# The third layer of four single experts as three passes of split fp32 in a fused attention and expert kernel

## The chip, the cores and the metric

The kernel runs on one core of a Trainium2 chip. The metric is the device time of one execution in microseconds: before the change, 740.17 us as the median of three runs (739.69 to 741.97).

## The reference

The input x is 2 x 2048 tokens of 512 values. Four blocks add to it in turn; the change touches the last.

```python
x = x + _L0_xattn_ref(_layernorm(x), ctx, ctx, mask, ...)   # cross attention with relu
x = x + _L0_ffn_ref(_layernorm(x), weight, bias)             # fp6-quantised product
x = x + _L1_xattn_ref(_layernorm(x), ctx, W, b)              # one 512x512 product and a mean
x = x + _L1_ffn_ref(_layernorm(x), Wg, bg, w1, b1, w2, b2, w3, b3)

def _L1_ffn_ref(x, Wg, bg, w1, b1, w2, b2, w3, b3):          # 16 experts
    probs = softmax(x @ Wg + bg, axis=tokens)
    vals, idx = top_k(probs per batch and expert, 128)
    tok = x[idx]                                             # 128 tokens per batch and expert
    h = relu(tok @ w1[e] + b1[e])
    h = relu(h @ w2[e] + b2[e])
    h = h @ w3[e] + b3[e]
    outputs.at[idx].add(h * vals)
```

Every expert is three 512x512 products on 128 tokens of each of the two batches, all in fp32 accuracy.

## The kernel before, in words

The first 410 us compute the three attention-like blocks tile by tile and the gate's logits; what follows are the experts. There are two kinds of work in the expert phase.

**Joint experts.** Twelve experts (numbers 4 to 15, called e = 0 to 11 in the code, `JOINT` of them) run with the tokens of both batches side by side, 256 columns. Each fp32 operand is split into a high and a low part of a reduced fp32 type (`F32R`): ScalarE writes the high part (`split_hi` for weights, line 1505; the second `activation` of `relu`, line 1907, for hidden values), VectorE subtracts it from the original for the low part (`split_lo`, `hidden_lo`, line 1982). A product is then `three_passes` (line 350): high by high, high by low, low by high, three matmuls for each of the four chunks of 128. The weights pass through a ring: the list `order` (line 504) names each weight matrix, `load_raw` brings item i of it into one of `RAW` = 3 raw buffers as soon as item i-3 has been split, and its halves go into `WR` = 5 pairs of buffers.

**Single experts.** Experts 0 to 3 have run already for one batch with unsplit fp32 matmuls. For the other batch they are put, one each, into the turns e = 1, 4, 7 and 9 (`SINGLE`, line 550): 128 tokens, three layers, all unsplit fp32 (`single_first`, `single_second`, `single_outputs`, lines 1409 to 1433). Their weights come into the buffers `w_e` by `load_single` (line 706) and are used as they land. `single_relu` (line 1914) on ScalarE makes the input of the next layer.

**Order of the work.** Nothing is scheduled by a planner; each engine runs its list in the order in which it is written, and semaphores tie the lists. TensorE in turn e: `single_tokens`, `hidden(e, 0)`, `single_first`, `tokens(e + 1)`, `outputs(e - 1)`, `single_second`, `hidden(e, 1)`, `single_outputs` (the four single parts only where e is in `SINGLE`). ScalarE in turn e: one weight split, the two relus of layer 0, `single_relu(.., 0)`, the tokens of e+1, a weight split, `single_relu(.., 1)`, a weight split, the relus of layer 1, `single_weighted`. VectorE in turn e: a weight split, `hidden_lo` twice, `token_lo(e + 1)`, then twice a weight split followed by `weighted(e - 1, b)`, then `hidden_lo` twice. `single_outputs` writes the bank that `weighted(e - 1, 1)` reads, so it waits for that (`d_y`, line 1428); the semaphore `a_sv` tells TensorE that ScalarE has made the single expert's values. GpSimd gathers tokens and adds results into the output with indirect DMAs; the program ends with the adds of e = 11.

Of the kernel before, what the change touches and what calls it, by code (L numbers as in the profile page):

```python
# [27 lines left out]
F32R = mybir.dt.float32r  # L28
# [4 lines left out]
ACT = mybir.ActivationFunctionType  # L33
AX_X = mybir.AxisListType.X

P = 128
# [9 lines left out]
FIRST = 4  # L46


def build(nc, io):
    B, S, D = io.x.shape  # L50
# [3 lines left out]
    C = D // P  # L54
# [28 lines left out]
        g_zero c_bcol k_full k_max k_top k_cand k_got k_half k_moved k_ids k_sum k_exp k_tr k_out k_pos a_soft  # L83
        a_w d_w g_w p_tok a_thi d_tlo a_h d_hlo p_h p_y d_y
        c_cut a_chain e_dve e_pe e_act e_pool e_logit
        p_ev a_ev p_sv a_sv s_gather
    """.split()
    sm = namedtuple("Semaphores", sem_names)(*[ctx.enter_context(nc.semaphore(n)) for n in sem_names])
    XR = 10
    RAW = 3  # L90
# [7 lines left out]
    sem_raw = [ctx.enter_context(nc.semaphore(f"raw_in{i}")) for i in range(RAW)]  # L98
# [9 lines left out]
    top = [-(-nc.sbuf_base // 64) * 64]  # L108

    def place(name, shape, dt=F32, at=None):  # L110

        size = int(np.prod(shape[1:])) * mybir.dt.size(dt)
        off = top[0] if at is None else at
        if at is None:
            top[0] = off + -(-size // 32) * 32
        return nc.alloc_sbuf_tensor_at(name, shape, dt, offset=off)
# [15 lines left out]
    b1 = place("b1", [P, E])  # L132
    b2 = place("b2", [P, E])
# [73 lines left out]
    KB = 1024  # L207
# [67 lines left out]
    w_h, w_l, w_raw = [], [], []  # L275
# [16 lines left out]
    h2_s = place("single_h2", [P, D], at=at_lists + 2 * KB)  # L292
# [2 lines left out]
    exps = place("exps", [P, GT])  # L295
    top[0] = at_qt
    tok_h, tok_l = place("tokT_h", [P, C, B * P], F32R), place("tokT_l", [P, C, B * P], F32R)
    tokT_s, h1_s = place("single_tokT", [P, D]), place("single_h1", [P, D])
    h32 = [place(f"h32_{i}", [P, 2 * B * P]) for i in range(2)]
    assert top[0] == at_x2  # L300
    for i in range(2, WR):
# [34 lines left out]
    def chunked(w):  # L336

        return w.rearrange("(c p) n -> p c n", p=P)
# [11 lines left out]
    def three_passes(pe, out, pairs):  # L350

        last = None
        n = 0
        for a_h, a_l, b_h, b_l in pairs:
            for a, b in ((a_h, b_h), (a_h, b_l), (a_l, b_h)):
                last = pe.matmul(out, a, b, start=(n == 0), stop=(n == 3 * len(pairs) - 1))  # L356
                n += 1
        return last
# [142 lines left out]
    GS = counts("half mean k01 k23 wf_0 wf_1 wf_2 wf")  # L501


    order = [(0, 0), (0, 1)]
    for e in range(1, JOINT):
        order += [(e, 0), (e - 1, 2), (e, 1)]
    order += [(JOINT - 1, 2)]
    when = {w: i for i, w in enumerate(order)}
    AHEAD = 3
# [37 lines left out]
    RING = (0, 1, 4, 2, 3)  # L547
    slots_in = ((sem_cut[0], 16 * (GB // 2) + 16), (sem_cut[1], 16 * (GB // 2) + 16), (sem_copies, 32), (sem_slots, 16))
    EV = counts("t0 t1 a0 a1 b0 b1 t2 y0 t3 y1 a2 a3 b2 b3 y2 y3")
    SINGLE = {1: 0, 4: 1, 7: 2, 9: 3}  # L550

    def first_adds(e):

# [21 lines left out]
    def used(eng, i):  # L575

        e, layer = order[i]
        if layer == 2:
            eng.wait_ge(sm.p_y, B * (e + 1))
        else:  # L580
            eng.wait_ge(sm.p_h, 4 * e + 2 * layer + 2)
# [5 lines left out]
    def _(sp):  # L587
# [110 lines left out]
        def load_raw(i):  # L698
            e, layer = order[i]
            if i >= RAW:  # L700
                sp.wait_ge(sm.a_w, i - RAW + 1)
                lo_done(sp, i - RAW)
            sp.dma_start(w_raw[i % RAW][:, :, :], chunked(io.w[layer][FIRST + e])).then_inc(sem_raw[i % RAW], 16)

        def load_single(s, layer):

            i = 3 * s + layer
            if i < 4:
                sp.wait_ge(sm.p_ev, EV["y3"])
            else:  # L710
                at, was = divmod(i - 4, 3)
                sp.wait_ge(sm.p_sv, 4 * at + was + 2)
            sp.dma_start(w_e[i % 4][:, :, :], chunked(io.w[layer][s])).then_inc(sem_early[i % 4], 16)

# [25 lines left out]
        for i in range(RAW + 1, len(order)):  # L740
            load_raw(i)
            for u, s in SINGLE.items():
                if i == max(when[(u, 0)], RAW + 1):
                    load_single(s, 0)
                    load_single(s, 1)
                if i == when[(u, 1)]:
                    load_single(s, 2)
        for b in range(B):
            sp.wait_ge(sem_add[b], 16 * E)

# [2 lines left out]
    def _(pe):  # L753
# [644 lines left out]

        def late_weights(s, layer):

            i = 3 * s + layer
            pe.wait_ge(sem_early[i % 4], 16 * ((3, 3, 2, 2)[i % 4] + i // 4 + 1))
            return w_e[i % 4]

# [19 lines left out]

        def single_outputs(s, u):

            w = late_weights(s, 2)
            pe.wait_ge(sm.d_y, B * u)
            pe.wait_ge(sm.a_sv, 4 * s + 3)
            for d in range(C):  # L1430
                last = pe.matmul(ps_y[1][:, :], h2_s[:, d * P:(d + 1) * P], w[:, d, :],  # L1431
                                 start=(d == 0), stop=(d == C - 1))
            last.then_inc(sm.p_sv, 1)

        def last_outputs():

# [30 lines left out]
        wh, _ = weights(0)  # L1467
# [27 lines left out]
    def _(act):  # L1495
# [392 lines left out]
        def token_hi(e):  # L1888
            for b in range(B):
                act.wait_ge(sm.p_tok, B * e + b + 1)  # L1890
                act.wait_ge(sm.p_h, max(0, 4 * (e - 1) + 2))
                for part in token_parts(e, b):
                    hi(sm.a_thi, tok_h[:, part, b * P:(b + 1) * P], in4(token_bank(e, b, part.start))[:, part, :])
# [20 lines left out]
        def single_relu(s, layer):  # L1914

            act.wait_ge(sm.p_sv, 4 * s + 2 + layer)
            act.activation((h1_s, h2_s)[layer][:, :], ps_hid[2 + layer][:, :], ACT.Relu,
                           bias=(b1, b2)[layer][:, s:s + 1]).then_inc(sm.a_sv, 1)

        def single_weighted(s, u):  # L1920

# [9 lines left out]
        for e in range(JOINT):  # L1931
            if nxt < len(order) and e > 0:
                split_hi(nxt)
                nxt += 1
            if e in SINGLE:
                single_copy(SINGLE[e])
            if e == 0:
                act.wait_ge(sem_add[0], 16 * 2)
            relu(e, 0, 0)
            relu(e, 0, 1)  # L1940
            if e in SINGLE:
                single_relu(SINGLE[e], 0)
            if e + 1 < JOINT:
                token_hi(e + 1)
            for n in range(2):
                if nxt < len(order) and (e > 0 or n == 1):
                    split_hi(nxt)
                    nxt += 1
                if n == 0 and e in SINGLE:
                    single_relu(SINGLE[e], 1)  # L1950
            if e == 0:
                act.wait_ge(sem_add[0], 16 * FIRST)
            relu(e, 1, 0)
            relu(e, 1, 1)
            if e in SINGLE:
                single_weighted(SINGLE[e], e)
# [4 lines left out]
    def _(dve):  # L1961
# [19 lines left out]
        def lo(sem, dst, src, hi_part):  # L1981
            dve.tensor_tensor(dst, src, hi_part, ALU.subtract).then_inc(sem, 1)  # L1982
# [554 lines left out]
        def split_lo(i):  # L2537
            dve.wait_ge(sm.a_w, i + 1)
            lo(sm.d_w, w_l[i % WR][:, :, :], w_raw[i % RAW][:, :, :], w_h[i % WR][:, :, :])

        def token_lo(e):
            for b in range(B):
                t = slice(b * P, (b + 1) * P)
                for i, part in enumerate(token_parts(e, b)):
                    dve.wait_ge(sm.a_thi, B * e + b + 1 + (i if e == 0 else 1))
                    lo(sm.d_tlo, tok_l[:, part, t], in4(token_bank(e, b, part.start))[:, part, :], tok_h[:, part, t])

        def hidden_lo(e, layer, pair):
            n = 4 * e + 2 * layer + pair
            dve.wait_ge(sm.a_h, n + 1)  # L2550
            src = h32[n % 2][:, :].rearrange("p (a t) -> p a t", a=2)
            part = slice(2 * pair, 2 * pair + 2)
            lo(sm.d_hlo, h_l[layer][:, part, :], src, h_h[layer][:, part, :])

        def weighted(e, b):

            dve.wait_ge(sm.p_y, B * e + b + 1)
            if e >= 2:
                dve.wait_ge(sem_add[b], 16 * (first_adds, second_adds)[b](e - 2))
            expert = FIRST + e  # L2560
            r = b * E + expert
            dve.tensor_scalar(y[e % 2][b][:, :], ps_y[b][:, :], b3[:, expert:expert + 1], vals[:, r:r + 1],  # L2562
                              ALU.add, ALU.mult).then_inc(sm.d_y, 1)
# [3 lines left out]
        nxt = 2  # L2567
        for e in range(JOINT):
            if nxt < len(order) and e > 0:
                split_lo(nxt)  # L2570
                nxt += 1
            hidden_lo(e, 0, 0)
            hidden_lo(e, 0, 1)
            if e + 1 < JOINT:
                token_lo(e + 1)
            for n in range(2):
                if nxt < len(order):
                    split_lo(nxt)
                    nxt += 1
                if e >= 1:  # L2580
                    weighted(e - 1, n)
            hidden_lo(e, 1, 0)
            hidden_lo(e, 1, 1)
        e = JOINT - 1
# [360 lines left out]
```

## Time and profile before

| what | value |
|---|---|
| median of three runs | 740.17 us (739.69 to 741.97) |
| the profiled execution | 738.98 us, of which the span is 737.2 us |
| TensorE busy | 714.1 us (97%) |
| VectorE busy | 520.4 us (71%) |
| ScalarE busy | 402.0 us (55%) |
| GpSimd busy | 421.6 us (57%) |
| granted TensorE clock, mean | 0.993 |

The span runs from the first instruction to the last of the profiled execution; 1.78 us of the execution lie around it. A row of a timeline has the start, the length, the engine (PE is TensorE, PEld its weight loads, DVE VectorE, ACT ScalarE, POOL GpSimd, SPq the queue of SyncE), the line of the kernel and the tiles (out<-in); in brackets stands idle time of the engine ahead of it and what ended it. Instructions on one engine overlap by a little, so the distance between two starts is shorter than the length. `banks` is the pair of accumulator banks 6 and 7, `early_w` the buffers `w_e`, and `single_h` the tiles `h1_s` and `h2_s`.

### The profile page before, as it was taken

The numbers are of one execution on the slowest core, as the hardware profiler recorded it, in microseconds if no ns is written. First come the engines' busy times: TensorE is split into PE (matmuls) and PEld (weight loads), VectorE is DVE, ScalarE is ACT, GpSimd is POOL, SyncE is SP. The second block draws the span as 40 slices with busy tenths as digits, with TensorE's granted clock in tenths as the row PEclk, the third lists the DMA queues.
The fourth block names the chain that finished last, engine by engine and source line by source line (L and its number), as shares of the span: only waits on it lengthen the run. The fifth ranks groups of instructions, "written<-read, shape, count | busy, mean of one in ns | idle before, by whom it ended". The sixth has DMA issues, their size and how long they took to land.

```text
span 737.2 us, 12752 instructions
## 1 busy us (share of the span) xinstructions
PE 714.1 (97%) x4506; PEld 623.2 (85%) x4506; DVE 520.4 (71%) x978; ACT 402.0 (55%) x680; POOL 421.6 (57%) x621
## 2 busy tenths in 40 slices
PE   6999999999999999999999899999999999999995
PEld 5765888888888888888888878798999899899894
DVE  5785789889888898875897798463664556363561
ACT  5755444454554445868668533454664556464641
POOL 2825789888888887876878722604430442340132
PEclk9999999999999999999999999999999999999998
DMA  8710122222212213110116998796895798995544
GB/s 311 267 30 15 44 73 76 76 85 73 89 60 87 86 58 103 44 61 29 61 60 242 334 401 296 191 366 186 234 372 165 192 355 268 298 274 157 143 86 58
DMA packets 61671, 118.04 MB, mean 160 GB/s; under 512 B 6056, under 2 KB 7464, under 8 KB 61608
## 3 DMA queue, kind: packets, MB, share of 16 engines
q1 hardware_dynamic: 54312, 100.44, 38.9%
q0 software_dynamic: 7296, 16.78, 10.3%
q8 instruction: 37, 0.61, 0.3%
q14 instruction: 26, 0.21, 0.1%
HBM read 91.76 MB, written 25.21 MB: 159 GB/s over the span
## 4 chain that ended last, share of the span: by engine, by line
PE 84%; issue 5%; DMA 3%; DVE 3%; POOL 2%; ACT 2%; POOLq 0%; DVEq 0%; ACTq 0%
PE bank L356 39%; PE banks L356 9%; PE bank L363 6%; PE bank L1004 6%; PE banks L871 4%; PE banks L877 3%; DMA out<-y,ids 3%; PE banks L1004 2%; PE banks L881 2%; PE banks L882 2%; PE banks L1431 1%; PE bank L1326 1%; PE banks L1035 1%; PE bank L1048 1%; DMA tok<-xn,ids 0%
## 5 line engine op out<-in xcount | busy, mean ns | idle before, releaser
L2851 POOL DMA_INDIRECT out<-y,ids x24 | 46.1, 1923 | 156.8 <-DVE y L2562 155.0
L1982 DVE TENSOR_TENSOR w_l<-w_raw,w_h 128x2048 fp32r<-128x2048 f32 x35 | 80.1, 2290 | 62.8 <-ACT w_h L1505 58.5
L1970 DVE BATCH_NORM_STATS2 bn<-x 128x6 f32<-128x512 f32 x112 | 77.0, 687 | 8.0 <-DMA x<-x 5.2
L1505 ACT ACTIVATE w_h<-w_raw 128x2048 fp32r<-128x2048 f32 x36 | 68.5, 1918 | 7.1 <-DMA w_raw<-w 7.1
L1901 ACT ACTIVATE h<-bank,b 128x512 f32<-128x512 f32 x48 | 33.1, 689 | 63.0 <-PE bank L356 60.0
L1982 DVE TENSOR_TENSOR hT_l<-h,hT_h 128x512 fp32r<-128x512 f32 x48 | 33.0, 690 | 40.3 <-ACT hT_h L1907 38.1
L356 PE MATMUL bank<-tokT_h,w_h 128*128 128x256 f32 x188 | 55.1, 293 | 0.0
L356 PE MATMUL bank<-tokT_h,w_l 128*128 128x256 f32 x188 | 53.2, 283 | 0.0
L356 PE MATMUL bank<-tokT_l,w_h 128*128 128x256 f32 x188 | 53.2, 283 | 0.0
L2614 POOL TENSOR_SCALAR rstd<-mean_var 128x1 f32<-128x1 f32 x108 | 25.9, 239 | 47.2 <-DVE mean_var L1975 42.2
L356 PE MATMUL bank<-wf_h,xdT_h 128*128 128x512 f32 x128 | 52.7, 412 | 0.0
L356 PE MATMUL bank<-wf_h,xdT_l 128*128 128x512 f32 x128 | 50.3, 393 | 0.0
L356 PE MATMUL bank<-hT_h,w_h 128*128 128x256 f32 x176 | 50.1, 285 | 0.0
L356 PE MATMUL bank<-wf_l,xdT_h 128*128 128x512 f32 x128 | 50.0, 390 | 0.0
L356 PE MATMUL bank<-hT_l,w_h 128*128 128x256 f32 x176 | 49.8, 283 | 0.0
L356 PE MATMUL bank<-hT_h,w_l 128*128 128x256 f32 x176 | 49.8, 283 | 0.0
L1659 ACT ACTIVATE q<-bank,bq 128x512 f32<-128x512 f32 x32 | 22.1, 689 | 45.0 <-PE bank L356 44.5
L2694 POOL TENSOR_TENSOR x<-x,mix_bias 128x512 f32<-128x512 f32 x32 | 41.4, 1293 | 1.9 <-PE bank L363 1.7
L2632 POOL TENSOR_TENSOR qT_l<-q,qT_h 128x512 fp32r<-128x512 f32 x32 | 41.5, 1297 | 0.8 <-ACT qT_h L1661 0.8
L2730 POOL TENSOR_TENSOR x<-x,ffn_bias 128x512 f32<-128x512 f32 x32 | 41.9, 1309 | 0.0
L1501 ACT ACTIVATE xn<-x,rstd 128x512 f32<-128x512 f32 x32 | 26.1, 816 | 24.6 <-POOL rstd L2629 19.6
L1982 DVE TENSOR_TENSOR xdT_l<-bank,xdT_h 128x512 fp32r<-128x512 f32 x32 | 22.0, 689 | 23.9 <-ACT xdT_h L1505 23.7
(426 smaller groups left out, 2377.3 us busy)
## 6 DMA issues: line engine op xcount, KB each, us to landing
w_raw<-w SPq DMA_DIRECT2D x36, 1024.0 KB
early_w<-w SPq DMA_DIRECT2D x24, 1024.0 KB, 10.6
x<-x SPq DMA_DIRECT2D x32, 256.0 KB, 2.8
xn<-xn SPq DMA_DIRECT2D x32, 256.0 KB
out<-x SPq DMA_DIRECT2D x29, 256.0 KB, 2.5
mask<-mask_t SPq DMA_DIRECT2D x8, 256.0 KB, 3.3
slot_all<-slots SPq DMA_DIRECT2D x4, 512.0 KB, 7.8
stage<-wk SPq DMA_DIRECT2D x1, 1024.0 KB, 7.8
```

What stands on the lines that cost most here:

```text
L356: last = pe.matmul(out, a, b, start=(n == 0), stop=(n == 3 * len(pairs) - 1))
L363: last = pe.transpose(bank[:, c * P:(c + 1) * P], src[:, c * P:(c + 1) * P], ident[:, :])
L871: last = pe.matmul(both_halves[:, a, 0:WIDE], xh[:, d, :], wc_h[:, d, a, :], start=(d == 0), stop=(d == C - 1))
L1004: last = pe.matmul(bank[:, c * P:(c + 1) * P], w[:, d, c * P:(c + 1) * P], x[:, d * P:(d + 1) * P], start=(d == 0), stop=(d == C - 1))
L1505: act.activation(dst, src, ACT.Copy).then_inc(sem, 1)
L1901: act.activation(h32[n % 2][:, :], ps_hid[n % 4][:, :], ACT.Relu, bias=bias)
L1970: dve.bn_stats(bn6[which][:, j % 2, :], src[:, :]).then_inc(sem_bn[which], 1)
L1982: dve.tensor_tensor(dst, src, hi_part, ALU.subtract).then_inc(sem, 1)
L2632: pool.tensor_tensor(dst, src, hi_part, ALU.subtract).then_inc(sem, 1)
L2694: pool.tensor_tensor(x2[j % 2][:, :], x2[j % 2][:, :], cbias[:, batch(j), :], ALU.add).then_inc(sm.g_x2b, 1)
L2730: pool.tensor_tensor(x1_of(k)[:, :], x1_of(k)[:, :], fbias[:, :], ALU.add).then_inc(sm.g_x1b, 1)
L2851: pool.indirect_dma_start(out=out_rows, out_offset=bass.IndirectOffsetOnAxis(ap=ids[:, r:r + 1], axis=0), in_=y[e % 2][b][:, :], in_offset ...
```

## The change

The third layer of the four single experts is computed by `three_passes` instead of four unsplit fp32 matmuls. Its weight matrix becomes an item of the ring's list, `(e, ALONE)`, just behind `(e, 1)`; the separate load of it goes, and `w_e` then holds two matrices for each single expert (`3 * s + layer` becomes `2 * s + layer` in `load_single` and `late_weights`, and the divisor there 2). ScalarE and VectorE each split one more matrix in each of the four turns. `single_relu(.., 1)` writes its result twice, as fp32 and as the high half, and the new `single_lo` on VectorE makes the low half. The two new tiles lie over `tokT_s` and `h1_s`, which are free by then. TensorE waits for `single_lo` by the new semaphore `d_sv`.

```diff
     tokT_s, h1_s = place("single_tokT", [P, D]), place("single_h1", [P, D])
+    h2_s_h = place("single_h2_h", [P, D], F32R, at=at_single)
+    h2_s_l = place("single_h2_l", [P, D], F32R, at=at_single + 2 * KB)
...
+    SINGLE = {1: 0, 4: 1, 7: 2, 9: 3}
+    ALONE = 3
     order = [(0, 0), (0, 1)]
     for e in range(1, JOINT):
         order += [(e, 0), (e - 1, 2), (e, 1)]
+        if e in SINGLE:
+            order.append((e, ALONE))
     order += [(JOINT - 1, 2)]
...
         e, layer = order[i]
-        if layer == 2:
+        if layer == ALONE:
+            eng.wait_ge(sm.p_sv, 4 * SINGLE[e] + 4)
+        elif layer == 2:
             eng.wait_ge(sm.p_y, B * (e + 1))
...
-            sp.dma_start(w_raw[i % RAW][:, :, :], chunked(io.w[layer][FIRST + e])).then_inc(sem_raw[i % RAW], 16)
+            w = io.w[2][SINGLE[e]] if layer == ALONE else io.w[layer][FIRST + e]
+            sp.dma_start(w_raw[i % RAW][:, :, :], chunked(w)).then_inc(sem_raw[i % RAW], 16)
...
                     load_single(s, 0)
                     load_single(s, 1)
-                if i == when[(u, 1)]:
-                    load_single(s, 2)
...
         def single_outputs(s, u):
 
-            w = late_weights(s, 2)
+            wh, wl = weights(when[(u, ALONE)])
             pe.wait_ge(sm.d_y, B * u)
-            pe.wait_ge(sm.a_sv, 4 * s + 3)
-            for d in range(C):
-                last = pe.matmul(ps_y[1][:, :], h2_s[:, d * P:(d + 1) * P], w[:, d, :],
-                                 start=(d == 0), stop=(d == C - 1))
-            last.then_inc(sm.p_sv, 1)
+            pe.wait_ge(sm.d_sv, s + 1)
+            f = [slice(d * P, (d + 1) * P) for d in range(C)]
+            three_passes(pe, ps_y[1][:, :], [(h2_s_h[:, f[d]], h2_s_l[:, f[d]], wh[:, d, :], wl[:, d, :])
+                                             for d in range(C)]).then_inc(sm.p_sv, 1)
...
             act.wait_ge(sm.p_sv, 4 * s + 2 + layer)
-            act.activation((h1_s, h2_s)[layer][:, :], ps_hid[2 + layer][:, :], ACT.Relu,
-                           bias=(b1, b2)[layer][:, s:s + 1]).then_inc(sm.a_sv, 1)
+            last = act.activation((h1_s, h2_s)[layer][:, :], ps_hid[2 + layer][:, :], ACT.Relu,
+                                  bias=(b1, b2)[layer][:, s:s + 1])
+            if layer == 1:
+                last = act.activation(h2_s_h[:, :], ps_hid[3][:, :], ACT.Relu, bias=b2[:, s:s + 1])
+            last.then_inc(sm.a_sv, 1)
...
             if e + 1 < JOINT:
                 token_hi(e + 1)
+            if e in SINGLE:
+                split_hi(nxt)
+                nxt += 1
             for n in range(2):
...
+        def single_lo(s):
+
+            dve.wait_ge(sm.a_sv, 4 * s + 3)
+            lo(sm.d_sv, h2_s_l[:, :], h2_s[:, :], h2_s_h[:, :])
+
...
             if e + 1 < JOINT:
                 token_lo(e + 1)
+            if e in SINGLE:
+                split_lo(nxt)
+                nxt += 1
             for n in range(2):
                 if nxt < len(order):
                     split_lo(nxt)
                     nxt += 1
                 if e >= 1:
                     weighted(e - 1, n)
+            if e in SINGLE:
+                single_lo(SINGLE[e])
             hidden_lo(e, 1, 0)
             hidden_lo(e, 1, 1)
```

On ScalarE, in turn e = 1 between the tokens of e = 2 and the relus of layer 1, before. `single_h_248` is the second layer's result of the single expert, `w_h` the high halves of weights, `w_raw` the ring's raw buffers.

```order
L1505 ACTIVATE tokT_h<-bank 128x4x128 [waits p_h,p_tok] x2
L1505 ACTIVATE w_h_226<-w_raw_229 128x2048 [waits p_h,raw_in2]
L1917 ACTIVATE single_h_248<-bank,b_64 128x512 [waits p_sv]
L1505 ACTIVATE w_h_228<-w_raw_225 128x2048 [waits p_h,raw_in0]
L1901 ACTIVATE h_0_257<-bank,b_64 128x512 [waits d_hlo,p_h]
L1907 ACTIVATE hT_h_222<-bank,b_64 128x512 [waits p_y]
```

The same place after the change:

```order
L1511 ACTIVATE tokT_h<-bank 128x4x128 [waits p_h,p_tok] x2
L1511 ACTIVATE w_h_226<-w_raw_229 128x2048 [waits p_h,raw_in2]
L1511 ACTIVATE w_h_228<-w_raw_225 128x2048 [waits p_h,raw_in0]
L1923 ACTIVATE single_h_248<-bank,b_64 128x512 [waits p_sv]
L1926 ACTIVATE single_h_h<-bank,b_64 128x512
L1511 ACTIVATE w_h_230<-w_raw_227 128x2048 [waits p_h,raw_in1]
L1907 ACTIVATE h_0_259<-bank,b_64 128x512 [waits d_hlo,p_h]
L1913 ACTIVATE hT_h_222<-bank,b_64 128x512 [waits p_y]
```

An instruction for `single_h_h` now stands between the single expert's relu and the split of the last weight matrix of the turn; the matrix that the single expert's third layer needs is split ahead of both (the first `w_h` of the second list).

On VectorE, in the same turn, before. `w_l` are the low halves of weights, `y` the scaled results of e = 0 for the two batches, `hT_l` the low halves of layer 1's values.

```order
L1982 TENSOR_TENSOR tokT_l<-bank,tokT_h 128x4x128 [waits a_thi] x2
L1982 TENSOR_TENSOR w_l_231<-w_raw_229,w_h_226 128x2048 [waits a_w]
L2562 TENSOR_SCALAR y_235<-banks,b_65,vals 128x512 [waits p_y]
L1982 TENSOR_TENSOR w_l_232<-w_raw_225,w_h_228 128x2048 [waits a_w]
L2562 TENSOR_SCALAR y_236<-banks,b_65,vals 128x512 [waits p_y]
L1982 TENSOR_TENSOR hT_l_224<-h_0_257,hT_h_222 128x512 [waits a_h]
L1982 TENSOR_TENSOR hT_l_224<-h_1_258,hT_h_222 128x512 [waits a_h]
```

After the change:

```order
L1994 TENSOR_TENSOR tokT_l<-bank,tokT_h 128x4x128 [waits a_thi] x2
L1994 TENSOR_TENSOR w_l_231<-w_raw_229,w_h_226 128x2048 [waits a_w]
L1994 TENSOR_TENSOR w_l_232<-w_raw_225,w_h_228 128x2048 [waits a_w]
L2579 TENSOR_SCALAR y_235<-banks,b_65,vals 128x512 [waits p_y]
L1994 TENSOR_TENSOR w_l_261<-w_raw_227,w_h_230 128x2048 [waits a_w]
L2579 TENSOR_SCALAR y_236<-banks,b_65,vals 128x512 [waits p_y]
L1994 TENSOR_TENSOR single_h_l<-single_h_248,single_h_h 128x512 [waits a_sv]
L1994 TENSOR_TENSOR hT_l_224<-h_0_259,hT_h_222 128x512 [waits a_h]
L1994 TENSOR_TENSOR hT_l_224<-h_1_260,hT_h_222 128x512 [waits a_h]
```

One more weight split stands ahead of the first `y`, and `single_h_l` stands behind the second `y`, that is, behind the split of the turn's last weight matrix. The same holds in the turns e = 4, 7 and 9.

## Rows read from the trace of the kernel before

**Rows 1.** The page: span, engine totals, granted clock in 40 slices (tenths).
```profile
span 737.2 us, 12752 instructions
PE 714.1 (97%) x4506; PEld 623.2 (85%) x4506; DVE 520.4 (71%) x978; ACT 402.0 (55%) x680; POOL 421.6 (57%) x621
...
PEclk9999999999999999999999999999999999999998
```

**Rows 2.** The chain that ended last: start us, length us, what; single expert 0's turn.
```profile
501.56 5.75 PE bank L356 x48
507.32 3.60 PE banks L1431 x8
...
517.54 5.46 PE banks L356 x24
```

**Rows 3.** Timeline, TensorE, entry into the single product: start, length, engine, line, operation.
```profile
507.04 0.28 PE L356 MATMUL bank<-hT_h,w_l 128*128 128x256 f32 x1
507.21 0.30 PEld L1431 LDWEIGHTS banks<-early_w,single_h 128*128 128x128 f32 x2
507.24 3.67 PE L1431 MATMUL banks<-early_w,single_h 128*128 128x512 f32 x8
```

**Rows 4.** Timeline, TensorE: first and twelfth of the 24 products of outputs(8).
```profile
668.63 0.47 PE L356 MATMUL banks<-w_h,hT_h 128*128 128x512 f32 x1
...
671.24 0.39 PE L356 MATMUL banks<-w_h,hT_l 128*128 128x512 f32 x1
```

**Rows 5.** Timeline, ScalarE, the same turn.
```profile
501.60 0.69 ACT L1917 ACTIVATE single_h<-bank,b 128x512 f32<-128x512 f32 x1 [6.45 <-PE bank L1004]
502.19 1.90 ACT L1505 ACTIVATE w_h<-w_raw 128x2048 fp32r<-128x2048 f32 x1
504.48 0.69 ACT L1901 ACTIVATE h<-bank,b 128x512 f32<-128x512 f32 x1 [0.39 <-PE bank L356]
```

**Rows 6.** Timeline, VectorE, the same turn.
```profile
504.12 2.29 DVE L1982 TENSOR_TENSOR w_l<-w_raw,w_h 128x2048 fp32r<-128x2048 f32 x1 [5.92 <-ACT w_h L1505]
506.33 0.81 DVE L2562 TENSOR_SCALAR y<-banks,b,vals 128x512 f32<-128x512 f32 x1
507.05 0.68 DVE L1982 TENSOR_TENSOR hT_l<-h,hT_h 128x512 fp32r<-128x512 f32 x1
```

**Rows 7.** Timeline, VectorE and TensorE, turn e = 4.
```profile
571.08 0.81 DVE L2562 TENSOR_SCALAR y<-banks,b,vals 128x512 f32<-128x512 f32 x1
...
571.96 0.30 PEld L1431 LDWEIGHTS banks<-early_w,single_h 128*128 128x128 f32 x2
```

**Rows 8.** Timeline and windows: a restart of TensorE behind VectorE.
```profile
468.66 0.41 DVE L1982 TENSOR_TENSOR tokT_l<-bank,tokT_h 128x256 fp32r<-128x256 f32 x1
...
469.18 0.19 PEld L1353 LDWEIGHTS bank<-tokT_h,w_h 128*128 128x128 f32 x1 [0.81 <-issue]
...
468.00:470.00 2.00, 1.60 (x11) 1.15 (x10) 1.95 (x4) 0.66 (x2) 1.70 (x3) 1.00 0.79 209
```

**Rows 9.** Timeline (SyncE, ScalarE) and windows: weight loads and where the queue runs empty.
```profile
523.56 1.05 SPq L713 DMA_DIRECT2D early_w<-w  x2
...
526.07 0.37 SPq L703 DMA_DIRECT2D w_raw<-w  x1
...
541.50 1.91 ACT L1505 ACTIVATE w_h<-w_raw 128x2048 fp32r<-128x2048 f32 x1 [2.91 <-DMA w_raw<-w]
...
552.15 0.37 SPq L703 DMA_DIRECT2D w_raw<-w  x1
...
557.00:562.00 5.00, 5.00 (x25) 4.15 (x24) 3.35 (x3) 2.90 (x4) 0.00 (x0) 1.00 0.13 49
```

**Rows 10.** Timeline, VectorE and GpSimd: the end of the program.
```profile
728.01 0.54 DVE L2590 TENSOR_SCALAR y<-bank,b,vals 128x256 f32<-128x256 f32 x1 [0.82 <-PE bank L1454]
728.83 1.54 POOL L2851 DMA_INDIRECT out<-y,ids  x1 [0.34 <-DVE y L2590]
```

More of the change, by code:

```diff
@@ L85, in build @@
         c_cut a_chain e_dve e_pe e_act e_pool e_logit
-        p_ev a_ev p_sv a_sv s_gather
+        p_ev a_ev p_sv a_sv d_sv s_gather
     """.split()
@@ L297, in build @@
     tok_h, tok_l = place("tokT_h", [P, C, B * P], F32R), place("tokT_l", [P, C, B * P], F32R)
+    at_single = top[0]
     tokT_s, h1_s = place("single_tokT", [P, D]), place("single_h1", [P, D])
+    h2_s_h = place("single_h2_h", [P, D], F32R, at=at_single)
+    h2_s_l = place("single_h2_l", [P, D], F32R, at=at_single + 2 * KB)
     h32 = [place(f"h32_{i}", [P, 2 * B * P]) for i in range(2)]
@@ L549, in build @@
     EV = counts("t0 t1 a0 a1 b0 b1 t2 y0 t3 y1 a2 a3 b2 b3 y2 y3")
-    SINGLE = {1: 0, 4: 1, 7: 2, 9: 3}
     def first_adds(e):
@@ L702, in load_raw @@
                 lo_done(sp, i - RAW)
-            sp.dma_start(w_raw[i % RAW][:, :, :], chunked(io.w[layer][FIRST + e])).then_inc(sem_raw[i % RAW], 16)
+            w = io.w[2][SINGLE[e]] if layer == ALONE else io.w[layer][FIRST + e]
+            sp.dma_start(w_raw[i % RAW][:, :, :], chunked(w)).then_inc(sem_raw[i % RAW], 16)
         def load_single(s, layer):
-            i = 3 * s + layer
+            i = 2 * s + layer
             if i < 4:
@@ L710, in load_single @@
             else:
-                at, was = divmod(i - 4, 3)
+                at, was = divmod(i - 4, 2)
                 sp.wait_ge(sm.p_sv, 4 * at + was + 2)
@@ L1399, in late_weights @@
         def late_weights(s, layer):
-            i = 3 * s + layer
+            i = 2 * s + layer
             pe.wait_ge(sem_early[i % 4], 16 * ((3, 3, 2, 2)[i % 4] + i // 4 + 1))
```

## The prediction

> **What bounds the kernel now.** I read the page first: TensorE is busy for 714.1 of 737.2 us, at the full clock in nearly every slice, with VectorE at 71% and ScalarE at 55% [rows 1]. Then the chain that ended last: around a single expert it goes from one group of TensorE's matmuls to the next with no other engine in it [rows 2]. So a microsecond less of matmuls there is a microsecond less at the end, as long as TensorE finds its operands ready; and a wait put ahead of TensorE costs all of itself. The question is which operand comes last in front of the single expert's third layer, so the third view is the timeline at that point.
>
> There the profile shows something that the totals hide. The last matmul of hidden(1, 1) starts at 507.04 us [rows 3], and they follow each other at 5.75 / 48 = 0.12 us [rows 2], so the next could start at 507.16. The first weight load of the third layer starts at 507.21 and its matmul at 507.24 [rows 3], after VectorE's second y, which ends at 506.33 + 0.81 = 507.14 [rows 6]. The same 0.07 us lies between y and the load in turn 4, 571.08 + 0.81 = 571.89 and 571.96 [rows 7]; the turns 7 and 9 repeat the pattern, four in all. TensorE thus already waits for y here, by some 0.08 us, once per single expert. The slack in this place is nothing; all four turns repeat it.
>
> **What TensorE saves.** The unsplit group takes 3.67 us from its first start to its last end [rows 3]. The new group is twelve matmuls of the form that outputs(e) has 24 of: 128x128 stationary, 512 columns, high and low halves. Its twelfth starts 671.24 - 668.63 = 2.61 us after the first and lasts 0.39 us, so twelve take 3.00 us from start to end [rows 4]. Saved: 0.67 us per single expert. By the chain's way of counting it is 3.60 - 5.46 / 2 = 0.87 us [rows 2], which leaves out the slower first matmul; since TensorE will restart from a wait, I take 0.67 and keep 0.87 as an end of the range.
>
> The Trainium skill ("FP8 and Floating Point Precision", TensorE Precision Notes) says that true fp32 makes four passes through the array; "TensorE: Matmul & The Clock Gate" (Back-to-back issue gap) gives N / 2.4 + 2.5 ns for one of them. By these the group goes from 16 passes to 12 of 0.216 us, 3.45 to 2.59 us, an estimated saving of 0.86 us. The trace agrees for the unsplit form (3.67 us), and shows the split form slower than the rule, 2.61 / 11 = 0.237 us per matmul. With the rule's figure the sum below would come out 0.8 us lower.
>
> **What the change puts in front of it.** TensorE now waits for d_sv, which VectorE gives after single_h_l. The order lists show single_h_l behind the second y, and that y is behind the low split of the turn's last weight matrix, which waits for ScalarE's high split, which is behind the single expert's relu. Step by step in turn 1:
> - ScalarE: the relu starts at 501.60, as before, since TensorE releases it. The next instruction started 0.59 us later [rows 5]. The added copy single_h_h takes that place, and the weight split moves from 502.19 to 502.78. It takes 1.90 and ends at 504.68.
> - VectorE: before, the low split started 504.12 - (502.19 + 1.90) = 0.03 us behind the high one; now at 504.71. y follows 506.33 - 504.12 = 2.21 us later, at 506.92, and the next instruction 507.05 - 506.33 = 0.72 us behind it [rows 6]. That is now single_h_l, at 507.64. It is the operation and shape of hT_l, 0.68 us [rows 6], and ends at 508.32.
> - TensorE: its weight load comes 0.07 us later, 508.39, and the first matmul 0.03 us after that, 508.42, instead of 507.24.
>
> So the start moves by 1.18 us: 0.59 for the copy on ScalarE and 0.59 for the subtraction behind y. The group then ends at 508.42 + 3.00 = 511.42 instead of 507.24 + 3.67 = 510.91. Each single expert costs 0.51 us more than before, though its matmuls are shorter. Nothing on TensorE behind it takes this back: it was busy from there to the next single expert, and the copy's delay of ScalarE is over when relu of layer 1 starts at 504.48 [rows 5] (the weight split, which ends at 504.68, makes it 0.2 us late at most, and nothing needs that relu before the next turn's outputs).
>
> **What is hidden.** The added weight split costs about 1.9 us on ScalarE and 2.2 on VectorE in each of the four turns. Both engines stood idle just there: 6.45 us ahead of the single relu [rows 5] and 5.92 us ahead of the low split [rows 6]. The extra split delays the first y by about 2.2 us, which goes into a GpSimd add and not to TensorE. These cost nothing. If the cover on VectorE were gone, the whole split would stand in the wait; it has 5.92 - 2.21 = 3.7 us to spare.
>
> **What the ring does.** One more item goes through it in each of these turns, and raw item i is asked for when item i-3 is split, so the loads behind the added one are asked for one place later. The tight one is the turn's last matrix, (e, 2): its load goes out when (e, 1) has been split. In turn 4, which is 571.08 - 506.33 = 64.75 us behind turn 1, a load is issued at that moment, 552.15, and ScalarE would want it at 502.78 + 64.75 = 567.53, 15.4 us later. The slowest landing I find is a load issued at 526.07 that ScalarE could use at 541.50, also 15.4 us [rows 9]. But that one had two matrices in the queue just ahead of it, issued from 523.56 on, and behind 552.15 the DMA engines are down to a share of 0.13 from 557 on [rows 9], so the load has landed about 5 us after its issue. With the separate load of the third layer gone, the queue holds no more than before. I cost it at 0, with 0 to 1 us per turn as bounds.
>
> **The sum.** 4 x (1.18 - 0.67) = +2.0 us. The end of the program hangs on TensorE: the last y ends at 728.55 and GpSimd's last add starts at 728.83, 0.34 us idle before it and released by that y [rows 10]; no single expert lies behind turn 9, so the tail moves as a whole. The profiled execution would go from 738.98 us (737.2 and 1.78 around it) to 741.0, and the median from 740.17 to 742.2. Bounds: with the chain's 0.87 the sum is 4 x 0.31 = 1.2 us. A restart of TensorE behind VectorE shows 469.18 - (468.66 + 0.41) = 0.11 us instead of 0.07 [rows 8]; with that, and 0.1 us more for the first matmul, and up to 0.1 for an instruction on ScalarE or VectorE that does not overlap, it is 4 x 0.75 = 3.0. The likeliest case alone is 741.4 to 743.2.
>
> **Rivals.**
> 1. No new wait: single_h_l is ready early and only y counts. Then the group starts at 507.16 to 507.24 and each single expert gains 0.67 to 0.87 us: 3.0 on the middle, 737.2 us. It needs the last weight split to be out of the way; the order lists speak against it. It could come true only if the releases worked otherwise than the rows say. Chance 0.07.
> 2. The ring runs dry: the load of (e, 2) lands more than 15.4 us after its issue, ScalarE's split of it waits, and behind it stand on the one line VectorE's low split, y, single_h_l and TensorE. From that point every microsecond of landing costs one, in each of four turns: at 16.4 us 4 more, 746.2 us. For it speaks the one landing of 15.4 us; against it the empty queue from 557 on. Chance 0.07.
> 3. The clock falls during the new waits. TensorE stood idle 0.81 us ahead of 469.18, and the window from 468 to 470 has a granted clock of 1.00 [rows 8], so a wait of 1.2 us should not do it. If it did, the 5.75 us of the next hidden layer [rows 2] would take twice as long once per turn: 23 us more, 765 us. Chance 0.01. The Trainium skill ("TensorE: Matmul & The Clock Gate", HAM oscillation) warns of TensorE idling for data between groups of matmuls, after which the gate throttles it again; the window from 468 to 470 does not show it.
>
> **How the numbers follow.** A measurement of this kernel can tell about 0.3%, 2.2 us, from no change. My case (chance 0.85) is +2.0 us, just inside that bound, and its own range goes over it: I give 0.50 of it to no change and 0.35 to slower. Faster is rival 1, 0.07. Slower is 0.35 + 0.07 + 0.01 = 0.43. The range goes from 740.4, below my bound of 741.4 for what the median of a few runs strays, to 744.2 on the side of rival 2.
>
> **What will show it.** In the trace after: TensorE idle by 1.1 to 1.2 us ahead of the first product of single_h_h in turns 1, 4, 7 and 9, released by single_h_l; single_h_l starting 0.7 us behind the second y; four groups of twelve matmuls of some 3.0 us; ScalarE's split of (e, 2) starting 1.2 us behind the single relu's start with no DMA wait. If TensorE runs through without idling there, rival 1 holds and the saving is real; if the waiting of w_h for w_raw has grown, rival 2; if the clock row has lower digits, rival 3. I would be wrong in the sum, not in the mechanism, if the wait is far from 1.18 us or the group from 3.0 us.

## The result, and the profile after

The changed kernel takes 742.54 us (median of 9 runs, 740.62 to 743.61), the kernel before 739.69 us beside it (9 runs). The ratio is 1.0026, 95% interval 1.0015 to 1.0038, that is +1.9 us (1.1 to 2.8). The two medians lie further apart, 2.85 us, at the upper end of that interval; in what follows the ratio is used. The interval lies above 1, so the change makes the kernel slower, but the ratio is inside the 0.3% that the prediction set as its bound for no change. The profiled execution took 741.43 us.

The page of the kernel after, its span and engine totals, answers to [rows 1]:

```profile
span 739.6 us, 12812 instructions
PE 710.6 (96%) x4522; PEld 625.1 (85%) x4522; DVE 533.2 (72%) x986; ACT 410.7 (56%) x688; POOL 420.2 (57%) x621
```

TensorE is busy for 3.5 us less than before (714.1 to 710.6), and yet the span is 2.4 us longer. Not all of the 3.5 us is the three passes' doing: two profiles of one kernel, split_first and split_first_again below, differ by 2.1 us in this number (711.7 and 709.6), and the turns below show 0.67 us less in each of four, 2.7 us. VectorE and ScalarE have 12.8 and 8.7 us more to do, most of it in time that they had.

The chain that ended last (start, length, what) in the turn of single expert 0, where the chain before had only TensorE [rows 2]:

```profile
502.61 0.68 ACT single_h_h L1926
503.29 1.81 ACT w_h L1511
505.13 2.29 DVE w_l L1994
507.42 0.72 DVE y L2579
508.14 0.61 DVE single_h_l L1994
508.75 0.14 issue
508.89 3.00 PE banks L359 x12
```

It leaves TensorE at the single expert's second relu and comes back to it through the copy, the weight split of ScalarE, VectorE's split, y and the subtraction, each behind the other: the line that the prediction laid out.

The timeline of ScalarE in that turn, for [rows 5]; the last row is the end of the single expert's turn:

```profile
502.02 0.69 ACT L1923 ACTIVATE single_h<-bank,b 128x512 f32<-128x512 f32 x1 [4.65 <-PE bank L1011]
502.61 0.68 ACT L1926 ACTIVATE single_h_h<-bank,b 128x512 fp32r<-128x512 f32 x1
503.18 1.92 ACT L1511 ACTIVATE w_h<-w_raw 128x2048 fp32r<-128x2048 f32 x1
...
511.93 0.78 ACT L1935 ACTIVATE single_y<-banks,single_bias,vals 128x512 f32<-128x512 f32 x1 [2.88 <-PE banks L359]
```

VectorE, for [rows 6]:

```profile
505.13 2.29 DVE L1994 TENSOR_TENSOR w_l<-w_raw,w_h 128x2048 fp32r<-128x2048 f32 x1 [4.30 <-ACT w_h L1511]
507.34 0.80 DVE L2579 TENSOR_SCALAR y<-banks,b,vals 128x512 f32<-128x512 f32 x1
508.06 0.68 DVE L1994 TENSOR_TENSOR single_h_l<-single_h,single_h_h 128x512 fp32r<-128x512 f32 x1
```

TensorE, for [rows 3] and [rows 4]: the last matmul of hidden(1, 1), the first weight load and matmul of the third layer, its second, and its twelfth matmul.

```profile
507.46 0.28 PE L359 MATMUL bank<-hT_h,w_l 128*128 128x256 f32 x1
...
508.86 0.19 PEld L359 LDWEIGHTS banks<-w_h,single_h_h 128*128 128x128 f32 x1 [1.32 <-issue]
508.89 0.47 PE L359 MATMUL banks<-w_h,single_h_h 128*128 128x512 f32 x1 [1.15 <-DVE single_h_l L1994]
509.19 0.39 PE L359 MATMUL banks<-w_l,single_h_h 128*128 128x512 f32 x1
...
511.50 0.39 PE L359 MATMUL banks<-w_h,single_h_l 128*128 128x512 f32 x1
```

The times are best counted from the start of the single expert's second relu, which TensorE alone releases: 501.60 before, 502.02 after. (The 0.42 us between them arise before this relu. In the ten profiles of the table below the relu starts anywhere from 501.60 to 505.60, at 504.07 in before_split_first, which has no part of the change; so I do not count them as its cost.) The first matmul of the third layer starts 6.87 us behind it, before 5.64 us: 1.23 us later. The group takes 511.50 + 0.39 - 508.89 = 3.00 us, before 3.67. (The profile shows each of the four unsplit matmuls as two records, hence x8 in [rows 3].) The turn is 0.56 us longer, and 4 x 0.56 = 2.24 us.

The list of waits in the expert phase has TensorE's new wait, four times, and ScalarE's waits for raw weights:

```profile
PE banks L359 <- DVE single_h_l L1994: 4.6, 4, 1.2
...
ACT w_h L1511 <- DMA w_raw<-w: 6.5, 2, 3.6
```

The 6.5 us of the second row were 6.3 us before, in two waits each time, and the granted clock keeps its digit 9 in every slice but the last. Neither rival 2 nor rival 3 shows.

### The profile page after: what moved, and what is told of

Its sections match the earlier page's. It is cut to its first block, busy times and chain, and to the rows that moved or that the text cites. A ratio compares the mean times of both kernels' runs of the same rounds, so it can differ in the third digit from the quotient of the medians.

```text
span 739.6 us, 12812 instructions
## 1 busy us (share of the span) xinstructions
PE 710.6 (96%) x4522; PEld 625.1 (85%) x4522; DVE 533.2 (72%) x986; ACT 410.7 (56%) x688; POOL 420.2 (57%) x621
## 4 chain that ended last, share of the span: by engine, by line
PE 76%; DVE 8%; issue 6%; DMA 3%; POOL 3%; ACT 2%; POOLq 0%; DVEq 0%; ACTq 0%
PE bank L359 36%; PE banks L359 11%; PE bank L366 6%; PE bank L1011 5%; PE banks L878 4%; PE banks L884 3%; DMA out<-y,ids 3%; PE banks L888 2%; PE banks L889 2%; DVE pack L2403 1%; DVE left L2413 1%; ACT w_h L1511 1%; PE bank L1333 1%; DVE pos L2405 1%; PE banks L1042 1%
## 5 line engine op out<-in xcount | busy, mean ns | idle before, releaser
L1994 DVE TENSOR_TENSOR w_l<-w_raw,w_h 128x2048 fp32r<-128x2048 f32 x39 | 88.9, 2289 | 58.0 <-ACT w_h L1511 47.7
L1511 ACT ACTIVATE w_h<-w_raw 128x2048 fp32r<-128x2048 f32 x40 | 75.8, 1919 | 8.0 <-DMA w_raw<-w 8.0
L359 PE MATMUL bank<-tokT_h,w_h 128*128 128x256 f32 x188 | 53.5, 285 | 0.0
```

Source lines behind the costliest of these rows:

```text
L1511: act.activation(dst, src, ACT.Copy).then_inc(sem, 1)
```

## The experiments

Theory W (the wait) is the prediction's, with the wait as measured: it costs 1.23 us per turn and the matmuls give back 0.67. Its rival R puts the loss on the ring, with four more weight matrices to load late and to split. The kernels under after were timed in two series, each beside runs of the kernel before: lo_first, no_lo_no_copy, ring_alone and split_first in one, the others in the second. In the table, "turn" is the time from the start of the single expert's second relu to the start of single_y in the first such turn, and "phase" is from that relu to the start of VectorE's last y, which holds all four turns; both come from one profile of each kernel. The last column is the ratio of times with its 95% interval.

| kernel | turn us | phase us | against before | ratio |
|---|---|---|---|---|
| before | 9.35 | 226.41 | | |
| after | 9.91 | 228.64 | +2.23 | 1.0026 (1.0015 to 1.0038) |
| lo_first | 9.41 | 226.70 | +0.29 | 1.0010 (0.9996 to 1.0023) |
| no_lo_no_copy | 8.83 | 224.36 | -2.05 | 0.9970 (0.9953 to 0.9988) |
| ring_alone | 9.50 | 227.05 | +0.64 | 1.0015 (1.0002 to 1.0029) |
| split_first | 8.51 | 223.06 | -3.35 | 0.9939 (0.9920 to 0.9957) |
| split_first_again | 8.50 | 223.05 | -3.36 | 0.9960 (0.9945 to 0.9974) |
| lo_first_y_last | 9.26 | 226.17 | -0.24 | 0.9992 (0.9977 to 1.0006) |
| before_split_first | 9.20 | 225.80 | -0.61 | 0.9994 (0.9983 to 1.0004) |
| two_copies | 10.46 | 230.86 | +4.45 | 1.0058 (1.0043 to 1.0072) |

The phase differs from that of before by four times the turn's difference, within 0.05 us (0.12 in lo_first_y_last), in every kernel, so the rest of the phase does not change. The four turns of one profile agree within 0.03 us in every kernel. That is why differences of 0.1 us per turn can be read here at all; the intervals of the times are 1.6 to 2.7 us wide, and by them alone lo_first, lo_first_y_last and before_split_first can't be told from the kernel before.

**lo_first.** VectorE makes the low half of the single expert's values before the last weight split:

```diff
             for n in range(2):
+                if n == 1 and e in SINGLE:
+                    single_lo(SINGLE[e])
                 if nxt < len(order):
                     split_lo(nxt)
                     nxt += 1
                 if e >= 1:
                     weighted(e - 1, n)
-            if e in SINGLE:
-                single_lo(SINGLE[e])
```

> Theory W (the wait): the change costs 1.23 us of waiting per single expert (0.58 for the copy single_h_h on ScalarE, 0.60 for single_h_l behind y, about 0.05 for the restart) and saves 0.67 us of matmuls. With single_h_l moved ahead of the last weight split on VectorE only the copy's 0.6 is left: TensorE waits about 0.6 us for y, and the kernel is at -0.1 to -0.4 us against the one before (2.2 us faster than the change). Rival R (the ring): the four added weight splits and the later loads cost the 2 us; then the order of single_h_l is of no account and this stays at +2 us.

The turn falls from 9.91 to 9.41 us: 1.9 us of the change's 2.2 are gone by reordering one instruction of 0.68 us. Rival R said +2 us and is out by the profile; the times (1.0010 beside 1.0026) point the same way with intervals that overlap. But W had -0.1 to -0.4 us, and the phase has +0.29. The rows of VectorE and of TensorE's weight load show where the rest is:

```profile
507.33 0.80 DVE L2579 TENSOR_SCALAR y<-banks,b,vals 128x512 f32<-128x512 f32 x1
...
508.36 0.19 PEld L359 LDWEIGHTS banks<-w_h,single_h_h 128*128 128x128 f32 x1 [0.83 <-issue]
```

y ends at 508.13 and the load starts at 508.36, a gap of 0.23 us. Before the change the same gap was 0.07 us [rows 3, 6].

**no_lo_no_copy.**

```diff
-            pe.wait_ge(sm.d_sv, s + 1)
+            pe.wait_ge(sm.a_sv, 4 * s + 3)
...
-            three_passes(pe, ps_y[1][:, :], [(h2_s_h[:, f[d]], h2_s_l[:, f[d]], wh[:, d, :], wl[:, d, :])
+            three_passes(pe, ps_y[1][:, :], [(h2_s_h[:, f[d]], h2_s_h[:, f[d]], wh[:, d, :], wl[:, d, :])
...
-            last = act.activation((h1_s, h2_s)[layer][:, :], ps_hid[2 + layer][:, :], ACT.Relu,
-                                  bias=(b1, b2)[layer][:, s:s + 1])
-            if layer == 1:
-                last = act.activation(h2_s_h[:, :], ps_hid[3][:, :], ACT.Relu, bias=b2[:, s:s + 1])
-            last.then_inc(sm.a_sv, 1)
+            act.activation((h1_s, h2_s_h)[layer][:, :], ps_hid[2 + layer][:, :], ACT.Relu,
+                           bias=(b1, b2)[layer][:, s:s + 1]).then_inc(sm.a_sv, 1)
...
-            if e in SINGLE:
-                single_lo(SINGLE[e])
```

> Leaves out the low half of the single expert's layer 2 result: ScalarE writes only the high half, VectorE makes no low half, and the twelve matmuls read the high half in its place; the ring and all weight splits stay. Theory W: TensorE starts as in the kernel before and saves its 0.67 us per single expert: -2.7 us against the kernel before. Rival R: the ring's cost stays, so the whole is at +2 us or, if the matmuls' saving had been masked by it, near 0.

The relu and single_y of ScalarE in the first turn, VectorE's y and TensorE's weight load:

```profile
503.49 0.69 ACT L1923 ACTIVATE single_h_h<-bank,b 128x512 fp32r<-128x512 f32 x1 [4.65 <-PE bank L1011]
...
512.32 0.78 ACT L1932 ACTIVATE single_y<-banks,single_bias,vals 128x512 f32<-128x512 f32 x1 [1.81 <-PE banks L359]
...
508.22 0.81 DVE L2576 TENSOR_SCALAR y<-banks,b,vals 128x512 f32<-128x512 f32 x1
...
509.25 0.19 PEld L359 LDWEIGHTS banks<-w_h,single_h_h 128*128 128x128 f32 x1 [0.25 <-issue]
```

The ring's four matrices are all there and the kernel is faster than before by 0.3% (0.1 to 0.5%), so four more matrices in the ring cannot be what makes the change slow. The phase says -2.05 us, not -2.7: each turn gives back 0.52 us instead of 0.67. The gap behind y is here too, from 509.03 to 509.25: 0.22 us where before had 0.07, and these 0.15 us are the difference.

**ring_alone.** The matmuls read the high half of the ring's weights as plain fp32. (The copy and single_lo, not shown in this cut, are removed as well.)

```diff
-            pe.wait_ge(sm.d_sv, s + 1)
-            f = [slice(d * P, (d + 1) * P) for d in range(C)]
-            three_passes(pe, ps_y[1][:, :], [(h2_s_h[:, f[d]], h2_s_l[:, f[d]], wh[:, d, :], wl[:, d, :])
-                                             for d in range(C)]).then_inc(sm.p_sv, 1)
+            pe.wait_ge(sm.a_sv, 4 * s + 3)
+            for d in range(C):
+                last = pe.matmul(ps_y[1][:, :], h2_s[:, d * P:(d + 1) * P], wh[:, d, :].bitcast(F32),
+                                 start=(d == 0), stop=(d == C - 1))
+            last.then_inc(sm.p_sv, 1)
...
```

> The third layer's weights go through the ring and are split, but the third layer runs in four unsplit fp32 matmuls on the high half of the weights (the low half is made and not read), with neither the copy nor single_h_l. Theory W: 0.0 us against the kernel before, within 0.5, as the splits lie in idle time. Rival R: +2 us.

ScalarE's relu and single_y, VectorE's y and TensorE's weight load:

```profile
501.82 0.69 ACT L1924 ACTIVATE single_h<-bank,b 128x512 f32<-128x512 f32 x1 [4.65 <-PE bank L1011]
511.32 0.78 ACT L1933 ACTIVATE single_y<-banks,single_bias,vals 128x512 f32<-128x512 f32 x1 [2.48 <-PE banks L1438]
...
506.55 0.80 DVE L2577 TENSOR_SCALAR y<-banks,b,vals 128x512 f32<-128x512 f32 x1
...
507.58 0.30 PEld L1438 LDWEIGHTS banks<-w_h,single_h 128*128 128x128 f32 x2 [0.25 <-issue]
```

Both theories miss. The phase is +0.64 us, the time +1.1 us (0.1 to 2.1). The turn is 9.50 instead of 9.35 us, and its 0.15 us lie in one place: y ends at 507.35 and the load starts at 507.58, 0.23 us instead of 0.07. VectorE's y itself stands where it stood, 4.73 us behind the relu in both kernels (506.55 - 501.82; 506.33 - 501.60). So the splits and loads of the ring are free, and what the route through the ring costs is 0.15 us per turn at TensorE's waits.

**lo_first_y_last.** What is it about the waits? The first matmul of the third layer in TensorE's list, with the semaphores that are asked for ahead of it, in three kernels (before, lo_first, and the new one). d_w and a_w say that the halves of the ring's weights are made, early_in2 that the separately loaded weights are in:

```
MATMUL banks<-early_w_214,single_h_248 128x512 [waits a_sv,d_y,early_in2]
MATMUL banks<-w_h_226,single_h_h 128x512 [waits d_y,d_sv,d_w,a_w]
MATMUL banks<-w_h_226,single_h_h 128x512 [waits d_sv,d_y,d_w,a_w]
```

The matmul itself carries the last one. The two ahead of it share one waiting instruction, and where there are four, the first has an instruction of its own. In lo_first, no_lo_no_copy and ring_alone that first one is d_y, the one that comes last in time. The new kernel swaps two lines of lo_first:

```diff
+            pe.wait_ge(sm.d_sv, s + 1)
             pe.wait_ge(sm.d_y, B * u)
-            pe.wait_ge(sm.d_sv, s + 1)
```

> As lo_first, but TensorE's list asks for d_sv before d_y instead of after it. In lo_first y was the last release and TensorE's weight load came 0.23 us behind y's end; in the kernel before, where d_y shares the last wait instruction ahead of the matmul, it came 0.07 us behind. Theory O (the order of waits): a release that a separate, earlier wait instruction asks for costs about 0.1 us more, since a second wait instruction follows it. Then the gap falls from 0.23 to 0.07 to 0.12 us and ScalarE's single relu to single_y from 9.41 to about 9.28 us, 0.5 us over four turns. Rival: the gap belongs to the number of waits (four instead of three), and stays at 0.23 us and 9.41 us.

VectorE's y and TensorE's weight load:

```profile
508.30 0.81 DVE L2579 TENSOR_SCALAR y<-banks,b,vals 128x512 f32<-128x512 f32 x1
...
509.22 0.19 PEld L359 LDWEIGHTS banks<-w_h,single_h_h 128*128 128x128 f32 x1 [0.72 <-issue]
```

y ends at 509.11, the load starts at 509.22: 0.11 us. The turn is 9.26 us, as expected. The number of waits is the same as in lo_first; only their order differs, and it is worth 0.15 us in the first turn and 0.11 to 0.15 in the others. Why an earlier wait costs more is not shown; that a second waiting instruction follows it fits, and no run parts it from other reasons.

**split_first.** The whole computation of the changed kernel, with one line of ScalarE's order changed:

```diff
             for n in range(2):
                 if nxt < len(order) and (e > 0 or n == 1):
                     split_hi(nxt)
                     nxt += 1
-                if n == 0 and e in SINGLE:
+                if n == 1 and e in SINGLE:
                     single_relu(SINGLE[e], 1)
```

> The whole computation of the changed kernel, with ScalarE's split of the turn's last weight matrix ahead of the single expert's second relu instead of behind it, in time in which ScalarE idles for 4.65 us. Theory W: VectorE has its low split, y and single_h_l done long before TensorE needs them, TensorE never idles there, and each single expert gains 0.75 us: -3.0 us against the kernel before, 5 us faster than the change. Rival R: +2 us as before. A second rival D (the load): the turn's last weight matrix has not landed by the earlier moment, ScalarE's relu waits for it, and the gain is part of that, between -3 and +2 us, with a DMA wait ahead of w_h in the trace.

The same kernel was run once more, as split_first_again:

> split_first a second time, beside the others on one chip: its trace put the four turns at -3.35 us in all, its times at -4.5 us (-5.9 to -3.2). If the trace's terms are all there is, the ratio comes out nearer to 0.9955 this time.

ScalarE's splits, relu and single_y; VectorE's single_h_l; TensorE's last matmul of hidden(1, 1), and the first two and the twelfth of the third layer:

```profile
494.00 5.53 ACT L1511 ACTIVATE w_h<-w_raw 128x2048 fp32r<-128x2048 f32 x3
502.37 0.69 ACT L1923 ACTIVATE single_h<-bank,b 128x512 f32<-128x512 f32 x1 [2.85 <-PE bank L1011]
...
510.88 0.78 ACT L1935 ACTIVATE single_y<-banks,single_bias,vals 128x512 f32<-128x512 f32 x1 [1.48 <-PE banks L359]
...
504.01 0.68 DVE L1994 TENSOR_TENSOR single_h_l<-single_h,single_h_h 128x512 fp32r<-128x512 f32 x1
...
507.81 0.28 PE L359 MATMUL bank<-hT_h,w_l 128*128 128x256 f32 x1
507.93 0.40 PE L359 MATMUL banks<-w_h,single_h_h 128*128 128x512 f32 x1
508.16 0.40 PE L359 MATMUL banks<-w_l,single_h_h 128*128 128x512 f32 x1
...
510.45 0.39 PE L359 MATMUL banks<-w_h,single_h_l 128*128 128x512 f32 x1
```

ScalarE does three weight splits in a row and still idles for 2.85 us before the relu: no load is late in this turn, and the other three turns are as short (8.50 to 8.51 us), so rival D is out. single_h_l ends at 504.69, over 3 us before TensorE wants it, and TensorE goes from one matmul to the next at 0.12 us. The turn is 0.84 us shorter than before, where 0.75 was expected; the twelve matmuls take 510.45 + 0.39 - 507.93 = 2.91 us, since the first one, which took 0.47 us behind a wait, now takes 0.40, and the second follows sooner. The two series of runs give 0.9939 and 0.9960; by the phase, -3.35 us, it should be 0.9955, inside the second interval and at the upper end of the first. This is the fastest kernel here, faster than before and after the change.

**before_split_first.** The same line is changed in the kernel before.

> The kernel before with nothing but ScalarE's split of the turn's last weight matrix moved ahead of the single expert's second relu. Theory W: it takes away only the 0.08 us that TensorE waits for y in each turn (and up to 0.08 us of a slower first matmul): -0.3 to -0.6 us against the kernel before, single relu to single_y from 9.35 to about 9.2 us. Rival: split_first owes its gain to the earlier split as such, in the joint experts' work; then this one gains 2 us or more without the three passes.

VectorE's second y and TensorE's first weight load of the unsplit third layer:

```profile
502.79 0.81 DVE L2562 TENSOR_SCALAR y<-banks,b,vals 128x512 f32<-128x512 f32 x1
...
509.51 0.31 PEld L1431 LDWEIGHTS banks<-early_w,single_h 128*128 128x128 f32 x2
```

y is done 5.9 us before the load, and the turn is 9.20 us, as expected. The reorder alone is worth 0.15 us per turn, the 0.08 of the wait and the slower first matmul. Of split_first's 0.84 us, 0.69 belong to the three passes. The rival for split_first, a gain of 2 us or more from the reorder alone, is out: the phase gives 0.61 us, and the times (0.9994, 0.9983 to 1.0004) exclude 2 us.

**two_copies.**

```diff
             if layer == 1:
+                act.activation(h2_s_l[:, :], ps_hid[3][:, :], ACT.Relu, bias=b2[:, s:s + 1])
                 last = act.activation(h2_s_h[:, :], ps_hid[3][:, :], ACT.Relu, bias=b2[:, s:s + 1])
```

> The changed kernel with a second copy of the single expert's values on ScalarE, ahead of single_h_h (into the tile that single_h_l overwrites). Theory W: ScalarE's split, VectorE's split, y, single_h_l and TensorE stand behind it in one line, so each turn is longer by the copy's 0.57 to 0.59 us: single relu to single_y from 9.91 to 10.49 us, 2.3 us more than the change and about +4.3 us against the kernel before. Rival R (the ring, or anything not in that line): no difference from the change, +2 us.

VectorE's single_h_l and TensorE's weight load:

```profile
512.21 0.68 DVE L1995 TENSOR_TENSOR single_h_l<-single_h,single_h_h 128x512 fp32r<-128x512 f32 x1
...
513.00 0.19 PEld L359 LDWEIGHTS banks<-w_h,single_h_h 128*128 128x128 f32 x1 [1.89 <-issue]
```

The load comes 0.11 us behind single_h_l, and the turn is 10.46 us, 0.55 more than after the change. So one more copy on ScalarE, an engine that is busy for little more than half of the span, costs TensorE nearly all of the 0.57 us that the copy takes on ScalarE.

## Why the prediction was right

- *TensorE bounds, and it already waits for y in this place.* Right, and before_split_first shows the second half: without that wait the turn is 0.15 us shorter.
- *The matmuls save 0.67 us behind a wait.* The group took 3.00 us as worked out. Some of that agreement is luck: the group of [rows 4] follows transposes with no idle time shown ahead of it, and its first matmul was slow (0.47 us) without a wait. Where the first matmul is not slow, in split_first, the group takes 2.91 us. Without a wait the saving is 0.69 us beside before_split_first, or 0.84 beside the kernel before with its wait. The Trainium skill ("FP8 and Floating Point Precision", TensorE Precision Notes) counts four passes for true fp32; the prediction's estimate of 0.86 us took that count, and for one pass the 0.216 us of the second page that it names. No pair of runs gives 0.86 us: the traces give 0.67 to 0.69 for the matmuls alone, since the split ones follow each other at 0.23 us and not at 0.216.
- *The wait costs 1.18 us.* It was 1.23. The parts were 0.57 for the copy (0.59 said: 503.18 - 502.61), 0.02 for a weight split that took 1.92 instead of 1.90 us, 0.60 for the subtraction (0.59 said), and the weight load came 508.86 - 508.74 = 0.12 us behind its release instead of 0.07. This is the mis-sized term. The 0.07 was read where d_y shares the last waiting instruction; in the changed kernel there are four waits in another arrangement. The upper bound had 0.11 us in it, from [rows 8].
- *The sum, +2.0 us.* The profile has +2.23 in the expert phase, the times +1.9 (1.1 to 2.8). The median was forecast at 742.2 us and came out at 742.54. That it counts as no change and not as slower is luck: the bound of 2.2 us lies inside the interval, as the prediction said of its own range.
- *The added splits and the later loads are free.* Right. ring_alone has them all, and VectorE's y is not later for it. The cost that ring_alone showed was not foreseen in any part: the route through the ring brings a fourth wait to TensorE and puts d_y first, 0.15 us per turn where y is what TensorE waits for. In the changed kernel y is not what ends the wait, so these 0.15 us did not come into the sum. Rival 2 did not show either.
- *Rival 1, no new wait, at 737.2 us.* It did not happen, but split_first builds it: 3.35 us less by the profile, where rival 1 had 3.0.

## What to carry to other kernels

Before a faster form of an instruction is credited with its saving, ask what it needs that the slower form did not, and behind what those new inputs stand in the list of the engine that makes them: here 0.67 us of matmul was bought with two small instructions that stood on the one line that TensorE waited for. The totals do not show such a line, since both engines had idle time left (VectorE was busy for 71% of the span, ScalarE for 55%); the few rows ahead of the bounding engine's instruction do. When the slack there is nothing, look at the order of work on the helper engines first: one moved line turned +2.2 us into -3.4 us in the profiles.

## What the runs showed of the hardware that was not expected

- The place of a wait in TensorE's list matters. From the release by VectorE to the weight load it took 0.22 to 0.23 us in three kernels (lo_first, ring_alone, no_lo_no_copy) where the late semaphore was asked for by the first of two waiting instructions, and 0.07 to 0.12 us where it stood in the last one ahead of the matmul (before, after, two_copies, lo_first_y_last).
- At the third layer, behind a wait, the first 512-column matmul takes 0.47 us and the next starts 0.30 us later (after); without a wait, 0.40 us and 0.23 us (split_first). A short wait in this place thus costs 0.07 us more than its length. But a wait is not the only thing that makes a first matmul slow. In the kernel before, the first product of outputs(8) takes 0.47 us and the next starts 0.31 us later, behind transposes and with no idle time shown ahead of it; what makes it slow was not tested:

```profile
668.27 0.60 PE L1326 MATMUL bank<-ident,tok 128*128 128x128 f32 x4
668.63 0.47 PE L356 MATMUL banks<-w_h,hT_h 128*128 128x512 f32 x1
668.94 0.39 PE L356 MATMUL banks<-w_l,hT_h 128*128 128x512 f32 x1
```
